# Score steps of self and cross attention joined on four row groups and four banks, in a new order of steps

## The reference

```
# self attention: 16 heads of 8, queries = keys = x
scores = einsum('bhtk,bhsk->bhts', y, y) / sqrt(8);  attn = softmax(scores)
o = einsum('bhts,bsc->bhtc', attn, x);  x1 = layernorm(x + o.reshape(b, t, 2048) @ weight)
# cross attention: 16 heads of 8, keys and values from ctx, window |i-j| <= 64
scores = einsum('bhqd,bhkd->bhqk', Q, K) / sqrt(8);  scores = where(mask, scores, -inf)
x2 = layernorm(x1 + softmax(scores) @ V ... @ Wo.T + bo)
# two local layers (8 heads of 64, l2 norm, rotary, window 64) each with a gated MLP
x3 = layernorm(x2 + ffn(x2))
```

## Time and profile before

| | |
|---|---|
| median of 3 runs | 1466.55 us (1461.12 to 1466.93) |
| profiled execution | 1461.15 us, of which the span of instructions is 1459.3 us |
| PE busy | 1333.5 us, 91% of the span, 12472 matmul records |
| DVE, ACT, POOL busy | 1026.3 us (70%), 938.5 us (64%), 885.3 us (61%) |
| granted TensorE clock | 0.965 on average |

### The profile page before, as it was taken

One profiled execution on the slowest core, in us unless ns is written; L12 is line 12 of the kernel. 1 busy time (PEld: TensorE's weight loads), 2 busy tenths in 40 slices (PEclk: granted clock), 3 DMA queues, 4 the chain that ended last, 5 costly groups with the idle time before them and its releaser, 6 DMA issues. The chain is left out here.

```text
span 1459.3 us, 39524 instructions
## 1 busy us (share of the span) xinstructions
PE 1333.5 (91%) x12472; PEld 928.8 (64%) x12472; DVE 1026.3 (70%) x2900; ACT 938.5 (64%) x2563; POOL 885.3 (61%) x1291
## 2 busy tenths in 40 slices
PE   5889999999999999999999999999999999998864
PEld 3556666666666666666666666666666666666543
DVE  2467776777777777777777777777777777776431
ACT  1256765677776667777766677776666777765552
POOL 2046666666666666666667666666666666666542
PEclk8799999999999999999999999999999999998785
DMA  5000000000000000000000000000000000000000
GB/s 158 10 5 4 5 7 7 5 4 5 4 4 5 5 5 5 4 4 4 5 5 5 5 5 4 4 4 5 5 5 5 4 5 3 5 5 3 3 3 4
DMA packets 22220, 12.55 MB, mean 9 GB/s; under 512 B 5878, under 2 KB 21024, under 8 KB 22176
## 3 DMA queue, kind: packets, MB, share of 16 engines
q1 hardware_dynamic: 21600, 10.96, 2.6%
q10 hardware_dynamic: 576, 1.05, 0.2%
HBM read 9.91 MB, written 2.10 MB: 8 GB/s over the span
## 5 line engine op out<-in xcount | busy, mean ns | idle before, releaser
L1212 POOL TENSOR_TENSOR local_e<-local_e,local_rd 128x512 f32<-128x512 f32 x128 | 133.0, 1039 | 238.2 <-DVE local_rd L1033 238.2
L848 ACT ACTIVATE local_e<-local_ps,local_bias,local_rn 128x128 f32<-128x128 f32 x512 | 230.8, 482 | 7.3 <-DVE local_bias L1029 7.3
L1191 POOL TENSOR_TENSOR local_rn<-local_sc,half_neg 128x8 f32<-128x8 f32 x128 | 211.3, 1658 | 14.4
L586 PE MATMUL self_ps<-self_z,self_e 128*128 128x129 f32 x1024 | 155.8, 291 | 2.6 <-ACT self_e L779 1.4
L1024 DVE TENSOR_REDUCE local_m<-local_ps 128x4 f32<-128x512 f32 x128 | 87.8, 686 | 96.4 <-PE local_ps L509 96.4
L586 PEld LDWEIGHTS self_ps<-self_z,self_e 128*128 128x128 f32 x1024 | 130.7, 196 | 13.8 <-issue 2.7
L955 DVE SCALAR_TENSOR_TENSOR self_y<-self_ps,self_rd,self_y 128x128 f32<-128x128 f32 x448 | 133.3, 345 | 8.8 <-issue 0.6
L606 PE MATMUL local_ps<-wz,self_kT 128*128 128x512 f32 x256 | 134.1, 627 | 1.1 <-ACT local_v L832 0.6
L848 ACT ACTIVATION_READ_ACCUMULATOR local_e<-local_ps,local_bias,local_rn 128x1 f32 x512 | 117.4, 229 | 0.0
L828 ACT ACTIVATE local_sq<-local_ps 128x512 f32<-128x512 f32 x128 | 76.1, 595 | 61.4 <-PE local_ps L665 58.4
L665 PE MATMUL local_ps<-wqkv_s,local_xT 128*128 128x512 f32 x128 | 71.4, 639 | 26.6 <-ACT local_xT L824 26.6
(11 more groups left out here) (172 smaller groups left out, 3392.6 us busy)
## 6 DMA issues: line engine op xcount, KB each, us to landing
self_xin<-x SPq DMA_DIRECT2D x32, 64.0 KB, 1.8
cross_cin<-ctx_in SPq DMA_DIRECT2D x32, 64.0 KB, 1.8
out<-local_out SPq DMA_DIRECT2D x32, 64.0 KB, 1.6
wqkv_s<-wqkv SPq DMA_DIRECT2D x2, 768.0 KB
wz<-w_heads ACTq DMA_DIRECT2D x4, 256.0 KB, 6.3
w_r<-w SPq DMA_DIRECT2D x2, 341.0 KB
con<-consts SPq DMA_DIRECT2D x1, 640.0 KB, 6.0
wo_s<-wo SPq DMA_DIRECT2D x2, 256.0 KB
```

The source lines that it names most:

```text
L586: last = nc.tensor.matmul(bank[:, 129 * j:129 * j + 129], s.e[:, h0 + j, :], s.z[:, h0 + j, :], start=True, stop=True)
L848: nc.scalar.activation(s.e[:, a, p, :], bank[:, 128 * p:128 * p + 128], ACT.Exp, bias=s.bias[:, a, p:p + 1], scale=s.rq[:, a, p:p + 1], ac ...
L1191: nc.gpsimd.tensor_tensor(s.rn[:, heads], s.sc[:, heads], half_neg[:, 0:LH], ALU.pow).then_inc(done, 8)
L1212: nc.gpsimd.tensor_tensor(s.e[:, a, :, :], s.e[:, a, :, :], s.rd[:, a, :].unsqueeze(2).to_broadcast([128, LH // 2, 128]), ALU.mult)\
```

## The change

`core16` goes. A new PE stage J, `joint_scores`, has its steps for self and cross attention together: step 1, 2, 5 and 6 each hold both attentions' matmuls for two groups, in turn, so that four row groups with four banks are in use; step 3 and 4 are the transpose of self and that of cross. A joint step waits for all that either of the two needs. The cross masks stand behind the matmuls of all four groups. The four order strings are new. What is computed, and every instruction's shape and type, stays.

```diff
 ORDER_TENSOR = (
-    "OONAAONASPBPABPBCZSCBZSZZASACSBBDCSECSSCSDSDSDCSDEEMCCECME")
+    "AONAOANOPPSBABPBCZCZBAAJDZJZJJBBJEJDSSDCCSSDCSSDEEMEME")
...
-            def head_scores(s, pair):
+            def head_scores(groups, w, n):
                 for j in range(GH):
-                    for g in pair:
+                    for s, g in groups:
...
-                if s.windowed:
-                    mask_band(s, pair, s.scores_n_psum)
+                if w is not None:
+                    mask_band(CROSS, CROSS.pairs[n], CROSS.scores_n_psum)
...
+            def joint_scores(v, w):
+                both = [s for s, u in ((SELF, v), (CROSS, w)) if u is not None]
+                pairs = [[(s, g) for s in both for g in s.pairs[n]] for n in range(2)]
...
+                head_scores(pairs[0], w, 0)
+                yield
+                if w is not None:
+                    pe.wait_ge(CROSS.max_done, w + 8)
+                if v is not None:
+                    pe.wait_ge(SELF.max_done, v + 8)
+                head_scores(pairs[1], w, 1)
+                yield
+                if v is not None:
+                    pe.wait_ge(SELF.max_done, v + STEP)
+                    nc.tensor.transpose(SELF.even.bitcast(BF16)[:, 0:128], SELF.neg[:, :], ident_b[:, :])\
+                        .then_inc(SELF.neg_psum, STEP)
+                yield
+                if w is not None:
+                    pe.wait_ge(CROSS.max_done, w + STEP)
+                    nc.tensor.transpose(CROSS.even.bitcast(BF16)[:, 0:128], CROSS.neg[:, :], ident_b[:, :])\
+                        .then_inc(CROSS.neg_psum, STEP)
+                yield
+                if w is not None:
+                    pe.wait_ge(CROSS.neg_ready, w + STEP)
+                if v is not None:
+                    pe.wait_ge(SELF.neg_ready, v + STEP)
+                turned_scores(pairs[0], w, 0)
+                yield
+                if w is not None:
+                    pe.wait_ge(CROSS.exp_done, w + 8)
+                if v is not None:
+                    pe.wait_ge(SELF.exp_done, v + 8)
+                turned_scores(pairs[1], w, 1)
+                yield
```

More of the change, by code:

```diff
@@ L417, in decoder_kernel, with stages @@
         N_PREP_P = 5
-        def stages(eng, order, prepare_local, self_stage, cross_stage, attention_head, attention_tail, mlp_head, mlp_tail, self_values=None):
+        def stages(eng, order, prepare_local, self_stage, cross_stage, attention_head, attention_tail, mlp_head, mlp_tail, joint_scores=None, self_values=None):
             def iteration(i):
@@ L428, in iteration @@
                     parts["C"] = cross_stage(at(i, SKEW["C"]))
+                if joint_scores is not None and (at(i, SKEW["S"]) is not None or at(i, SKEW["C"]) is not None):
+                    parts["J"] = joint_scores(at(i, SKEW["S"]), at(i, SKEW["C"]))
                 for l in range(2):
@@ L521, in head_scores, with turned_scores @@
                             last.then_inc(s.scores_n_psum, 4)
-                if s.windowed:
-                    mask_band(s, pair, s.scores_n_psum)
-            def turned_scores(s, pair):
-                for g in pair:
+                if w is not None:
+                    mask_band(CROSS, CROSS.pairs[n], CROSS.scores_n_psum)
+            def turned_scores(groups, w, n):
+                for s, g in groups:
                     rows = slice(32 * g, 32 * g + 32)
@@ L537, in turned_scores @@
                             last.then_inc(s.scores_t_psum, 4)
[L538 to L543, removed]
+                if w is not None:
+                    mask_band(CROSS, CROSS.pairs[n], CROSS.scores_t_psum)
+            def joint_scores(v, w):
+                both = [s for s, u in ((SELF, v), (CROSS, w)) if u is not None]
+                pairs = [[(s, g) for s in both for g in s.pairs[n]] for n in range(2)]
+                if v is not None and not again(v):
@@ L544, in core16 @@
                     pe.wait_ge(made_first, 2)
-                    if s.windowed:
+                if w is not None:
+                    if not again(w):
                         pe.wait_ge(prep_p, N_PREP_P)
[L547 to L550, removed]
-                yield
-                pe.wait_ge(s.max_done, v + 8)
-                head_scores(s, s.pairs[1])
+                    pe.wait_ge(CROSS.k_ready, w + STEP)
+                    pe.wait_ge(CROSS.low, w + STEP)
+                    pe.wait_ge(CROSS.q_wide, w + STEP)
@@ L554, in core16 @@
+                if v is not None:
+                    pe.wait_ge(SELF.k_ready, v + STEP)
+                    pe.wait_ge(SELF.low, v + STEP)
+                    pe.wait_ge(SELF.q_wide, v + STEP)
+                head_scores(pairs[0], w, 0)
+                yield
+                if w is not None:
[3 more added lines that the diff above has]
+                head_scores(pairs[1], w, 1)
                 yield
-                pe.wait_ge(s.max_done, v + STEP)
@@ L560, in core16 @@
                 yield
-                pe.wait_ge(s.exp_done, v + 8)
-                turned_scores(s, s.pairs[1])
+                if w is not None:
+                    pe.wait_ge(CROSS.neg_ready, w + STEP)
[3 more added lines that the diff above has]
+                yield
+                if w is not None:
+                    pe.wait_ge(CROSS.exp_done, w + 8)
+                if v is not None:
+                    pe.wait_ge(SELF.exp_done, v + 8)
```

14 lines of the change are left out of this document (4 added, 10 removed).

## The result

| | before | after |
|---|---|---|
| median of 5 runs | 1461.55 us (1460.59 to 1466.93) | 1477.71 us (1471.79 to 1478.12) |
| ratio, 95% interval | | 1.0084 (1.0064 to 1.0105) |
| profiled execution's span | 1459.3 us | 1470.0 us |
| one iteration of the loop at 2.4 GHz | 42.00 us | 42.17 us |
| PE busy, whole run | 1333.5 us | 1269.7 us |

The forecast of no change was wrong: the kernel is slower by 16 us between the two medians, beyond the 7 us that its measurement tells from nothing. The ratio is taken over all runs and is smaller than the quotient of the two medians (1.011); by it the loss is 12 us.

The account below looks back on a forecast made before the run. PE was taken to bound the loop: work falls from 40.1 to 37.0 us per period, but 5.25 us of waits bring it to 42.0, as before. Forecast 1462 us, no difference, own range 1455 to 1469, with rivals 1420 to 1492.

Parts of the forecast that it names:

- rival 3: Joint steps: four row groups don't run at once; 1480 us if only bf16 parts need longer, 1533 with float32; chance 0.10.
- The walk: One round of the loop's new order on all engines, adding hand-overs and waits; closes at a 42.0 us period.
- rival 1: Loop waits smaller than walked, sign a sum under 4 us: period 40.8, 1424 us, far end 1365; chance 0.38.
- 5.25 summed: Sum in us of ten PE waits in one loop period, put on top of 37.0 us of PE work.
- J1: First joint step of the loop iteration, forecast to start at 15.6 us after ten PE steps without a gap.
- time 0: Start of layer 1's output projection, PE's last step of the loop, from which forecast times are counted.
- Rival 2: Loop's head: ScalarE's table load starts later, delaying gelu, gate and output product; period 42.6, 1480 us; chance 0.22.
- The clock won't move it: Whole run: granted clock stays at 2.4 GHz, as new waits are 1.1 us or shorter and spread over the period.
- not walked and may add 5 us either way: Filling and draining, 11 of 37 iterations, were left out of the count; their effect put at up to 5 us.
- 31 x 0.0 to 0.2: Loop: 31 iterations with both attentions, each 0.0 to 0.2 us longer, giving 1461 to 1467 us.

Follow-up runs that it names:

- all three cut: Changed kernel without gelu and its table loads, maxima over half the keys, GpSimd's q and k inverse roots replaced by a product of constants: 1415.13 us, ratio 0.967.
- the pairs in turn: Changed kernel with self's pair of row groups issued first and cross's behind it in every joint step: 1602.24 us, ratio 1.0887.
- the filled wait: Changed kernel plus an unread 512-column product between the transposes of self and cross maxima: 1466.21 us, ratio 1.0029; added to the pairs in turn, 1509.79 us.

## Why the prediction was wrong

**What held.** Four row groups run at once: a joint first step in 0.34 us for 0.33 to 0.36 forecast, 0.96 in float32 for 0.96 to 1.0. The Trainium skill's 25 ns floor between starts ("TensorE: Matmul & The Clock Gate", "Wait — 56ns, not 53.3ns?") does not hold across row groups here: 719.18, 719.19, 719.24, 719.26; rival 3 falls. PE busy is 38.05 of 42.17 us for "37 to 38.5". The walk found the waits where they are: L574 1.1 forecast and 0.98 measured, L569 0.4 and 0.35, L699 0.3 and 0.24, L531 0.65 and 0.62, L730 0.6 and 0.41, L752 0.8 and 1.01; L771, 0.75 and 0.38, is the one that is far off. The measured ones are gaps, which sum to 94.3 / 24 = 3.9 us in an iteration. By its letter that is the sign of rival 1, "under 4 us", but the forecast counts from start to start, and there 42.17 less 37.0 of work leaves 5.2 for the 5.25 summed. J1 starts 15.8 us after time 0 for 15.6. That several chains end close together was shown by cutting them, and it is closer than I wrote: three, not two. Rival 1's period, 40.8, came only with all three cut, at 40.99. Rival 2 had the direction right, but not its mechanism: the gelu ends 4.0 us after layer 1's projection for 4.1 forecast (703.39 to 707.41), L683 doesn't wait, and taking the table loads away leaves the period at 42.18.

**The step that failed first** is "The clock won't move it". I took it from 20 us of the filling with PE busy for 16.1 and a granted clock of 1.00, and from each new wait being 1.1 us or shorter. That one stretch said nothing of waits that follow one another, nor were the new waits spread over the period, as the sentence has it: three of them stand within 2 us. In the loop of the profiled execution the clock cost 3.3 us and in the filling 5.0 of 7.5; one product that fills the place takes the ratio from 1.0084 to 1.0029. No rival of mine was the clock.

**The second** is the sentence on filling and draining, "not walked and may add 5 us either way". They were worth +7.5 and -4.3, +3.2 in sum; as a bound on the sum it held, but both terms are as large as the loop's, and the granted clock of the filling before, 0.93 on average over 245 us, would have said that the clock moves there; the prediction rests on 20 us of it.

**The third** is a size. The walk closed at 42.0 us, measured 42.17, and "31 x 0.0 to 0.2" gives 5.3 us for 0.17. It held inside its range, but the forecast took the lower end, 1462, from it.

Together: 4.2 (period) + 3.3 (clock in the loop) + 7.5 (filling) - 4.3 (draining) = 10.7 us between the profiled executions; I had 0.9. Filling and draining cancel in part. That the period came out so near, 42.0 for 42.17, is partly luck: L771 and L752 err by 0.4 and 0.2 in opposite directions.

**What stays open.** Why the median of after lies 5.9 us above its profiled execution. Why the pairs in turn, with more work on PE in a period and the same places of waiting, lose so much more to the clock than the joint steps (0.91 and 0.93 in the loop, where these have 1.00 in the same view); the filled wait cures both, and no run tells how much each of the three waits of that place has to do with it. Fewer waits there are not always better: without L699's, in the kernel without table loads, six stretches at 1.2 GHz stand in the loop for three. And whether the 1.2 us of the last cut is all from the transposes. A kernel with only the inverse roots cut was not run.

## What to carry to other kernels

Steps of two attentions joined on an engine with one list of instructions save its time and give up the cover that each had from the other: before such a change, count not only the work saved but what stands between producer and consumer afterwards, and how many engines' chains end at that place, since here a gain came only when the last of them was shortened. Where a change opens several waits of TensorE close together, try an unread product in them, and measure the mean granted clock of the filling and the loop apart. And try each phase of a schedule by itself: here the draining alone was a small gain, 0.2%, that the sum hid. Before a variant is read as "without the change", see in its rows that it is: the pairs in turn took out two thirds of it.

## What the chip showed that I had not expected

- Matmuls on four groups of 32 rows with four banks start some 10 to 20 ns apart and a round of four takes the time of a round of two: bf16 of 128 columns 0.34 us for sixteen (0.32 for eight), float32 of 512 columns 0.96 us for eight records (0.96 for four).
- For that the matmuls need not be issued in turn. With eight of two row groups ahead of eight of two others in the program, the later eight start among the earlier (477.38, 477.41, 477.44 us) and all sixteen take 0.36 us; the matmuls of PE's list don't start strictly in its order, where the text ahead of the prediction says that each engine works in order.
- In a loop where no wait of PE is over 1.0 us, the granted clock fell to 1.2 GHz for a few us at a time, in three iterations of the profiled execution; with the pairs in turn for up to 17 us of an iteration. Every one of these stretches starts behind the same place, where waits of 0.35, 0.98 and 0.24 us lie within 2 us; none starts behind the other wait of 1.0 us. The Trainium skill says in "TensorE: Matmul & The Clock Gate", section "A second HAM failure mode: psum-queue depth-cycling", that short idle spots between groups of matmuls, if frequent, let the clock swing between its two levels; the traces agree, with the waits just named.
- More work made the kernel faster: 64 unread matmul records (12536 for 12472), ratio 1.0029 for 1.0084.
